# A gather convolution with a routed two-expert layer: the main loop issued in steps of two tiles

## The reference, cut to what matters

```python
wave = (x @ wave_w.T + wave_b).reshape(Bx, Lx, H, 2)
freq = MIN_FREQ + jax.nn.sigmoid(wave[..., 0]) * (MAX_FREQ - MIN_FREQ)
phase = jnp.tanh(wave[..., 1]) * freq
offs = phase[..., None] + freq[..., None] * taps
pos = jnp.clip(jnp.arange(Lx)[None, :, None, None] + offs, 0.0, Lx - 1)
i0f = jnp.floor(pos); frac = pos - i0f
gathered = g0 + frac[..., None] * (g1 - g0)      # rows i0 and i0 + 1 of x, by head
kmat = (x @ kernel_w.T + kernel_b).reshape(Bx, Lx, H, K)
w = jnp.take_along_axis(kmat, bins, axis=3)      # bins = clip(floor((offs + 256) / 512 * 64))
y = jnp.einsum('blhs,blhsd->blhd', w, gathered).reshape(Bx, Lx, Cx)
return y @ out_w.T
```

## Time and profile before

| | |
|---|---|
| median of three runs | 1327.14 us |
| profiled execution | 1334.1 us, span 1332.0 us |
| TensorE matmuls | 1143.9 us busy, 86% of the span |
| VectorE | 859.9 us, 65% |
| ScalarE | 788.1 us, 59% |
| GpSimd | 588.7 us, 44% |
| granted TensorE clock | 0.955 of full speed in the mean |

### The profile page before, as it was taken

The page is one execution under the profiler, slowest core; times in us unless marked ns, Lnnn a source line. Parts: engine busy times, 40 slices in busy tenths (PEclk is TensorE's granted clock), DMA queues, the critical chain, the costliest instruction groups (busy, mean ns, idle before and its releaser), DMA issues. The chain is left out here.

```text
span 1332.0 us, 34891 instructions
## 1 busy us (share of the span) xinstructions
PE 1143.9 (86%) x11855; PEld 743.6 (56%) x11855; DVE 859.9 (65%) x2508; ACT 788.1 (59%) x1650; POOL 588.7 (44%) x838
## 2 busy tenths in 40 slices
PE   4699999999999999999999999999923989999840
PEld 2366656666666666666666666666611556565520
DVE  4477777787787778778777867777661333333336
ACT  2476676677667667766766776676501555555520
POOL 4233155346337435634733562442436545544520
PEclk9999999999999999999999999999956999999975
DMA  5546456446545544655654554544412442222237
GB/s 179 157 124 175 109 151 167 122 133 185 139 129 174 157 120 137 183 139 135 176 148 119 159 146 127 144 139 116 153 63 70 143 128 69 73 69 73 67 144 256
DMA packets 213179, 179.82 MB, mean 135 GB/s; under 512 B 147600, under 2 KB 183184, under 8 KB 212368
## 3 DMA queue, kind: packets, MB, share of 16 engines
q1 hardware_dynamic: 204336, 159.68, 43.3%
q0 software_dynamic: 8672, 17.92, 4.1%
HBM read 95.42 MB, written 82.12 MB: 133 GB/s over the span
## 5 line engine op out<-in xcount | busy, mean ns | idle before, releaser
L1325 DVE SCALAR_TENSOR_TENSOR aw<-ps,ks 128x64 f32<-128x64 f32 (+7 forms) x960 | 379.9, 435 | 207.8 <-PE ps L1015 170.6
L794 ACT ACTIVATE ps<-ps,f 128x512 f32<-128x512 f32 x512 | 342.4, 669 | 233.5 <-PE ps L1006 233.4
L1021 PE MATMUL ps<-ident,aw 128*128 128x128 f32 x2048 | 335.0, 287 | 36.2 <-ACT att L802 15.5
L1021 PEld LDWEIGHTS ps<-ident,aw 128*128 128x128 f32 x2048 | 217.3, 142 | 163.3 <-issue 124.5
L623 POOL COPY kn<-kn 128x256 f32<-128x256 f32 x64 | 25.5, 398 | 425.4 <-DVE kn L1309 425.4
L1011 PE MATMUL ps<-cn,ptt 32*128 32x512 bf16 x512 | 199.3, 389 | 3.5 <-ACT ps L794 3.5
L1015 PE MATMUL ps<-cn,ptt 32*128 32x512 bf16 x512 | 199.2, 389 | 0.0
L1006 PE MATMUL ps<-cp,ptt 32*128 32x512 bf16 x512 | 198.4, 390 | 0.0
L1335 DVE COPY att<-ps 128x512 f32<-128x512 f32 x256 | 175.7, 686 | 20.1 <-PE ps L1021 13.8
L724 POOL DMA_INDIRECT y_scratch<-aw,idu x135 | 129.3, 958 | 129.7 <-ACT aw L886 128.5
L802 ACT ACTIVATE att<-ps 128x512 f32<-128x512 f32 x256 | 151.8, 593 | 14.3 <-PE ps L1021 14.2
(11 more groups left out here) (177 smaller groups left out, 1695.8 us busy)
## 6 DMA issues: line engine op xcount, KB each, us to landing
k_scratch<-kn SPq DMA_DIRECT2D x64, 512.0 KB, 4.1
ka<-e_scratch SPq DMA_DIRECT2D x64, 512.0 KB, 3.4
ks<-k_scratch SPq DMA_DIRECT2D x128, 130.0 KB
e_scratch<-kr SPq DMA_DIRECT2D x128, 126.0 KB, 3.4
dl<-slot_scratch SPq DMA_DIRECT2D x135, 65.0 KB, 1.8
att<-y_scratch SPq DMA_DIRECT2D x16, 512.0 KB, 5.2
xc<-in_x SPq DMA_DIRECT2D x8, 512.0 KB, 6.3
h_scratch<-hx SPq DMA_DIRECT2D x16, 256.0 KB, 4.3
```

Of the source, the lines that this page charges most:

```text
L794: act.activation(ps_s[T % BANKS][:, :], ps_s[T % BANKS][:, :], ACT.Relu, scale=f27[:, i % 2, r, h:h + 1]).then_inc(s_e, 1)
L1021: last = nc.tensor.transpose(bank[:, j * P:j * P + P], aw[:, T % RING, j * P:j * P + P], ident[:, :])
L1325: ins = nc.vector.scalar_tensor_tensor(dst[:, a:b, :], src[:, a:b, :], -TAPS * SCALE, rows(ks[:, R % 2, h, o:o + 1], [[0, b - a], [1, HP]] ...
```

## The change

It issues the loop in steps of two tiles. `RING` becomes 4. At an even h TensorE now issues the count strips of T + 2 and T + 3, the gap strips of T + 4 and T + 5, the undo strips of T + 2 and T + 3, then turn T, and in the next iteration turn T + 1 with no strips ahead of it. Counts move from h = 0 to h = 1, behind the weigh, and the edge turns from h = 2 and 4 to h = 3 and 5, the second behind the weigh. VectorE weighs T + 2 in iteration T, and evicts the odd tile T before it weighs T + 2. ScalarE's gap ramp is one tile further ahead, and its evictions of counts and edges move with their units.

```diff
-RING = 3
+RING = 4
@@ unit_order
-        if h == 0 and R + 1 < NR:
+        if h == 1 and R + 1 < NR:
             order.append(("count", R + 1))
-        if h == 2:
+        if h == 3:
             order.append(("edge", R, 0))
-        if h == 4:
+        if h == 5:
             order.append(("edge", R, 1))
@@ ScalarE
-            for T in range(BANKS - 1):
+            for T in range(BANKS):
                 gap(T)
...
-                if T + BANKS - 1 < NT:
-                    gap(T + BANKS - 1)
+                if T + BANKS < NT:
+                    gap(T + BANKS)
                 if h % 2 == 0:
                     tile_evicted(T)
-                if h == 0 and R + 1 < NR:
+                if h == 1 and R + 1 < NR:
                     counted(R + 1)
-                if h == 2:
+                if h == 3:
                     edge_evicted(R, 0)
                 if h == 3 and R:
                     copied(R - 1)
-                if h == 4:
+                if h == 5:
                     edge_evicted(R, 1)
@@ TensorE
-                if T + 1 < NT:
-                    undone_on(T + 1)
-                if T + 2 < NT:
+                if h % 2 == 0 and T + 2 < NT:
                     tile_on(T + 2)
-                if T + BANKS - 1 < NT:
-                    gap_on(T + BANKS - 1)
+                    tile_on(T + 3)
+                    if T + BANKS < NT:
+                        gap_on(T + BANKS)
+                        gap_on(T + BANKS + 1)
+                    undone_on(T + 2)
+                    undone_on(T + 3)
                 turn_tile(T)
-                if h == 0 and R + 1 < NR:
-                    counts(R + 1)
                 if h == 1 and R:
                     weigh(R - 1, 1)
-                if h == 2:
-                    turn_edges(R, 0)
+                if h == 1 and R + 1 < NR:
+                    counts(R + 1)
                 if h == 3 and R + 2 < NR:
                     bins(R + 2)
-                if h == 4:
-                    turn_edges(R, 1)
+                if h == 3:
+                    turn_edges(R, 0)
                 if h == 5:
                     weigh(R, 0)
+                    turn_edges(R, 1)
@@ VectorE
+            for T in range(2):
+                weighted(T)
             for T in range(NT):
...
-                weighted(T)
-                if T and h % 2 == 0:
-                    tile_evicted(T - 1)
+                if h % 2:
+                    tile_evicted(T)
+                if T + 2 < NT:
+                    weighted(T + 2)
...
-            tile_evicted(NT - 1)
```

More of the change, by code:

```diff
@@ L1094, in _ @@
             counts(0)
-            for T in range(BANKS - 1):
+            for T in range(BANKS):
                 gap_on(T)
-            tile_on(0)
-            undone_on(0)
-            tile_on(1)
+            for T in range(2):
+                tile_on(T)
+            for T in range(2):
+                undone_on(T)
             for b in range(2):
```

## The result

The changed kernel takes 1354.77 us (median of four runs, 1349.92 to 1357.57) against 1327.73 us for the kernel before beside it. The ratio is 1.0196, 95% interval 1.0161 to 1.0231: **2.0% slower**, by some 27 us. The forecast was 1337, slower, with a range of 1316 to 1358. Sign and range held, but the range only just: the forecast had a loss of 10 us and the measured one is 27, so the loss was underrated by some 18 us.

A forecast was written before the change was run, and what follows sets the result against it. TensorE led before; after, VectorE's chain of eviction and weighing binds most steps. A pair takes 117.2 us against 115.4; six give +11, first and last pair -1, so +10 on 1327.14: 1337, range 1316 to 1358.

The forecast's parts named there:

- VectorE's cycle: Main loop: odd eviction, odd weighing, then gap and undo strips and turns form a chain, 2.91 us between second turns.
- P0: Two-tile step from second turn at h = 1 to h = 3, with counts: TensorE alone 2.90 us, VectorE's cycle 2.91.
- P3: Step from second turn at h = 7 to h = 1 of the next R: TensorE alone 2.19 us, VectorE's cycle 2.91.
- P1: Step from second turn at h = 3 to h = 5, with bins and edges: TensorE alone 2.96 us, with VectorE 3.10.
- TensorE's paths: TensorE's own time through the four steps of an R: 11.2 us in sum, against 12.7 measured before.
- P2: Step from second turn at h = 5 to h = 7, with weigh and edges: 3.12 us, TensorE's own path.
- The rival of four row groups that don't run at once: TensorE's strips: a fourth row group costs 0.21 us a step, 54 at most, 1390; within a shared 0.15 chance.
- Mode switches: TensorE between turns and strips: up to 0.1 us each, in the sums; the skill's rule alone gives a 10 to 25 gain.
- Side turns: Between the turns of P3 in r = 2 to 6: second turn waits 0.97 us longer, 4.8 a pair.
- Centring: ScalarE, r = 1 and 2: activations delay ramps, even eviction and edge turn by 2.0 and 2.2 us; +2.1 a pair.
- Large side products: Outputs, wave product, gate scores and ranks, issued between the two turns, lengthen VectorE's cycle in full: 7.8 us a pair.
- VectorE's other work: Sums, spreads and top-two choice on VectorE, partly in free time: 4.0 us a pair, 2.3 of it in r = 4.

The follow-up runs named there:

- both experiments: Two runs on the changed kernel: VectorE weighs before evicting the odd tile, ratio 0.9913; a memset added between odd eviction and odd weighing, 1380.61 us.
- weighing first: The changed kernel, but VectorE weighs T+3 before it evicts the odd tile T+1: 1319.63 us, ratio 0.9913.
- The early reads: The changed kernel, but VectorE reads the side bank at h = 1 of r = 3 to 6, not h = 2: 1332.67 us, ratio 1.0013.
- ramps first: The changed kernel, but ScalarE does both ramps of a step before the even eviction: 1390.70 us, ratio 1.0447.

## Why the prediction was right, and where it fell short

**VectorE's cycle** (forecast 2.91 in P0 and P3, 3.10 in P1): right for P3 and P1. In R's without other waits the trace has 2.86 to 3.00 in P3 and 3.1 to 3.2 in P1, and both experiments moved these two. P0 has its 2.89, but not from this cycle alone: TensorE's own path is at least as long (2.90), and breaking the cycle left P0 where it was. For the sum that makes no difference; that the forecast's two values for P0 lay 0.01 apart is what hid it. This was the step that turned an expected gain of TensorE's (11.2 against 12.7 an R) into 0.6, and r = 7 shows it: 12.70, 12.15, 11.34 for before, change and weighing first. By the Trainium skill, TensorEngine Tiling (Array Packing), PSUM Bottleneck, the reading of the banks may become the limit when strips are packed; the trace agrees in kind (TensorE's gap strips wait 33.9 us for VectorE in 300:900), but the price of its rule as I had made it, 50 us, did not come: it is 27.

**TensorE's paths:** right. P2 3.16 against 3.12, undo after count 0.22 against 0.21. The rival of four row groups that don't run at once is gone. The Trainium skill, TensorE: Matmul & The Clock Gate, Part 3, has four at once, and the trace agrees: all four take 0.39 from nearly one start.

**Mode switches:** by the Trainium skill, TensorEngine Tiling (Array Packing), Key Properties, a change of tiling mode drains the array, which would give a gain from half the blocks. With the cycle broken, r = 7 is 1.36 shorter than before, and switches are part of it; no run takes them by themselves.

**Side turns** (+0.97): right in size. The second turn is 1.43 behind the first, +0.94, and moving them gave 0.64 to 0.97 where nothing stood behind. The prediction puts this into P3; the side turn of h = 6 stands between the turns of h = 6 and 7, at the end of P2, and there the trace has it: 4.10 in place of 3.16.

**Centring** (2.0 and 2.2 over the steps alone): 2.0 and 1.9 in the trace of the change, as worked out above.

**Large side products** (in full between the turns): right in size. From turn to turn it is 2.20 against 0.49 for wave product and scores, +1.7; outputs add 2.0 and the ranks 0.2, 7.7 a pair in all against 7.8.

**VectorE's other work, the term that failed.** The forecast took 4.0 us a pair for all of it, as time ahead of the eviction. In pairs at full clock it is about 5.5: that is what r = 0, 3, 4, 5 and 6 take beyond the forecast's other terms. It missed who else waits. TensorE's next product into the same bank, bins at h = 3, would come 0.44 after the second turn, and VectorE reads the old one behind weighing and edge terms. That stops TensorE before the edge turn and the next strips. With the read alone added to the 3.10 of P1 (start to start 0.20 for the wave product, 0.34 for the ranks, 0.60 for the output sum) P1 would be 3.30, 3.44 and 3.70 in r = 3, 5 and 6; it is 3.73, 3.80 and 4.13. The early reads took away 3.5 a pair. Before, the same reads had room: bins starts 0.46 to 0.50 behind its turn in every R, and no wait of it for VectorE stands in the view of 300:900.

**The rest of the gap.** In three of the six middle pairs of the change the clock falls in r = 4: P0 takes 4.44 there, not 2.93, and the pair 119.7, not 118.6. The trace of before has three such pairs as well, 0.9 to 1.3 longer than its 115.1. So the falls cost both kernels about the same, and the change costs 3.5 a pair without them. Over the six pairs the traces differ by 21.6 (from the first turn of the second pair to that of the last), 11 more than forecast. The first pair is 2.0 shorter and the last 1.0 longer, together the -1 that I gave them: in the start-up the edge turn's wait for its end terms (L1028 on L636) is 4.1 long where it was 8.7. Behind the last turn, where the change touches nothing, the change is 0.8 shorter; the other kernels differ there by more. The remaining 7 us, by which the gap of the medians is larger than that of the traces, come from the profiled execution of before, which lay 6 us above its median. Most of that is seen beside the trace with the fourth buffer alone (1328.36 us): there the main loop from 70 us on has one fall of the clock where before has four, and the part behind the last turn is 1.6 shorter. Why the falls come isn't settled.

**The rivals.** The faster one (slack enough) falls with VectorE's cycle. "ScalarE closes the cycle" did not happen in plain steps: r = 7 shows no such wait, and it kept its 12.14 even with both ramps ahead of the eviction. ScalarE sets the step only where side turns or centring stand in it, as *ramps first* shows. "Near balance" is out by the interval. That the range held owes something to its width: VectorE's cycle was right, and one wait beside it was missing from a term, which came to 5.5 in place of 4.0 a pair.

## What to carry to other kernels

When an order is coarsened from one tile to two, write down for each engine which instruction of the step comes last and who waits for it. Here the odd eviction ahead of the odd weighing made a chain through two engines that no busy share shows. What each step is held by is read step by step: of four steps this chain held two. For each step that moves, look too at every bank it shares with rare work: the next user of a bank moved earlier, and the reader of the last one did not. And edits that are good alone have to be run together, because each one shortens the time in which others hid, and their traces are compared pair by pair, since falls of the clock can cover a gain.

## What the runs showed of the hardware

Four strips on four row groups start within 0.01 us and all take 0.39, as three did in the kernel before (602.68 and 602.69). A second strip on a row group follows the first by 0.22 (510.90 to 511.12). In r = 4 of the fifth pair of the change, behind the gate scores, TensorE's granted clock was at half (the lower of its two levels, 1.2 GHz) for 3.4 us, as the view of windows shows (TensorE, weight load, VectorE, ScalarE and GpSimd busy, then the clock, DMA share, GB/s):

```profile
504.30:516.50 12.20, 11.75 (x153) 7.60 (x150) 10.08 (x24) 8.87 (x16) 5.40 (x8) 1.00 0.49 142
576.40:579.80 3.40, 3.40 (x41) 1.72 (x42) 1.37 (x4) 0.98 (x2) 2.91 (x5) 0.50 0.77 151
```

The array was busy all the time in it, and for 3.34 us of the 3.4 before it. Four such falls lie between 70 us and the end of the main loop in the trace of before and four in that of the change, at other times; the weigh of that stretch took 1.94 us where it takes 1.08. A pair with one is 0.9 to 1.3 us longer than its neighbours without. A memset of 192 columns on VectorE between two others costs 0.21 us, more than the 0.14 of it that shows from its start to the next one's, because the instruction ahead of it no longer overlaps: the memset starts at its end (589.34 + 0.69 to 590.02), where the weighing used to start 0.08 before that.
